# Attention scores from two float32r parts, two heads at a time on half of TensorE's rows, in a fused attention and expert-attention kernel

## The reference

```
x = x + attn(layernorm(x)):
    q, k, v = x @ Wq.T, x @ Wk.T, x @ Wv.T          16 heads of 16 features
    softmax(q k^T / 16) v, per head, then @ Wo.T + bo
x = x + ffn(layernorm(x)):                           8 heads of 64 features, 5 experts
    wv = top2mask(x Ws) * sigmoid(x Ws);  v = sum_e wv_e (x Wv_e)
    softmax(q k^T / 8) v, per head
    out = sum_e top2mask(x Wd)_e (attn Wo_e)
```

## Time and profile before

| | us |
|---|---|
| runs | 6238.3, 6242.69 (median 6240.49) |
| profiled execution | 6241.76 |
| its span | 6239.9 |
| granted TensorE clock, mean | 0.877 of full speed |
| busy PE / PEld / DVE / ACT / POOL | 5111.2 / 2215.6 / 3996.4 / 2947.7 / 3752.6 |

### The profile page before, as it was taken

How to read it: one execution, slowest core, us unless ns; L and a number is a source line. 1 busy time by engine, 2 the same in 40 slices (tenths; PEclk the granted TensorE clock), 3 DMA queues, 4 the chain that set the end, 5 groups by cost and what they waited for, 6 DMA issues and landing times.

```text
span 6239.9 us, 62744 instructions
## 1 busy us (share of the span) xinstructions
PE 5111.2 (82%) x20352; PEld 2215.6 (36%) x20352; DVE 3996.4 (64%) x6573; ACT 2947.7 (47%) x5313; POOL 3752.6 (60%) x3078
## 2 busy tenths in 40 slices
PE   5778888888888888888888888888888888888876
PEld 1233333333333333333333333333333333333333
DVE  4466666666666666666666666666666666666542
ACT  1344444544544544544544544544545444545542
POOL 0046656666656666656666656666656666656688
PEclk7689888989888989889989889989889989889887
DMA  2111111111111111111111111111111111111000
GB/s 67 44 33 42 34 28 41 38 28 39 36 28 38 41 28 37 39 28 37 42 28 37 39 28 37 42 28 35 40 28 37 41 29 34 42 28 34 18 8 7
DMA packets 151479, 213.70 MB, mean 34 GB/s; under 512 B 23408, under 2 KB 125104, under 8 KB 150960
## 3 DMA queue, kind: packets, MB, share of 16 engines
q1 hardware_dynamic: 151152, 209.69, 12.6%
HBM read 139.87 MB, written 69.73 MB: 34 GB/s over the span
## 4 chain that ended last, share of the span: by engine, by line
PE 43%; DVE 22%; POOL 12%; issue 11%; ACT 11%; DMA 0%; SPq 0%; POOLq 0%; ACTq 0%; DVEq 0%
PE bank L190 8%; PE bank L214 6%; POOL s_acc L726 5%; DVE s_mxa L681 4%; PE bank L224 4%; PE bank L276 4%; PE bank L202 4%; DVE s_mxf L693 3%; PE bank L343 3%; ACT s_pa L496 3%; POOL s_vh L744 3%; DVE s_xn L597 3%; DVE s_xn L542 3%; PE bank L332 2%; DVE s_k L642 2%
## 5 line engine op out<-in xcount | busy, mean ns | idle before, releaser
L496 ACT ACTIVATE s_pa<-bank 128x512 f32<-128x512 f32 x2048 | 1227.2, 599 | 2054.2 <-PE bank L214 2051.1
L681 DVE TENSOR_REDUCE s_mxa<-bank 128x1 f32<-128x512 f32 x2048 | 1389.1, 684 | 935.3 <-PE bank L224 930.1
L726 POOL TENSOR_TENSOR s_acc<-s_pf 128x512 f32<-128x512 f32 x256 | 326.9, 1278 | 1375.5 <-PE bank L363 1250.7
L214 PE MATMUL bank<-s_qs,s_ks 99*128 99x512 bf16 x2048 | 858.5, 419 | 329.0 <-ACT s_pa L496 323.0
L726 POOL TENSOR_TENSOR s_acc<-s_acc,s_pf 128x512 f32<-128x512 f32 x512 | 650.7, 1277 | 680.3 <-ACT s_pf L509 678.6
L224 PE MATMUL bank<-s_ks,s_qs 96*128 96x512 bf16 x2048 | 862.6, 421 | 227.7 <-DVE s_mxa L681 195.3
L190 PE MATMUL bank<-s_pa,s_v 128*17 128x512 f32 x4096 | 686.3, 748 | 305.4 <-DVE s_t L569 235.9
L509 ACT ACTIVATE s_pf<-bank 128x512 f32<-128x512 f32 x1024 | 611.6, 597 | 415.6 <-PE bank L237 227.7
L693 DVE TENSOR_REDUCE s_mxf<-bank 128x1 f32<-128x512 f32 x1024 | 698.4, 683 | 140.3 <-PE bank L254 138.6
L214 PEld LDWEIGHTS bank<-s_qs,s_ks 99*128 99x128 bf16 x2048 | 200.5, 98 | 1633.8 <-issue 983.2
L768 POOL TENSOR_TENSOR s_uu<-s_uu,s_pu 128x640 f32<-128x640 f32 x448 | 695.5, 1552 | 35.1
(11 more groups left out here) (98 smaller groups left out, 7110.5 us busy)
## 6 DMA issues: line engine op xcount, KB each, us to landing
w_parts<-s_pt SPq DMA_DIRECT2D x128, 384.0 KB, 2.8
s_ks<-w_parts SPq DMA_DIRECT2D x768, 64.0 KB, 2.9
s_qs<-w_parts SPq DMA_DIRECT2D x128, 192.0 KB, 3.6
s_xn<-in_x SPq DMA_DIRECT2D x32, 512.0 KB, 5.0
s_qs<-w_parts SPq DMA_DIRECT2D x128, 128.0 KB, 3.7
s_xa<-in_x SPq DMA_DIRECT2D x32, 512.0 KB, 4.3
out_y<-s_xa SPq DMA_DIRECT2D x32, 512.0 KB, 3.0
s_qs<-w_parts SPq DMA_DIRECT2D x128, 64.0 KB, 3.6
```

Source lines behind the costliest of these rows:

```text
L214: e.matmul(bk[:, :], ks[0:99, c, h, 128 * kc:128 * kc + 128], qs[0:99, c, h, :], start=True, stop=True).then_inc(p_aexp, 1)
L496: e.activation(pa[:, k % 6, :], Xa.at["x", b, n, g][:, :], ACT.Exp, scale=0.0625).then_inc(a_aexp, 1)
L681: e.tensor_reduce(mxa[:, c, g, h:h + 1], Ma.at["m", b, n, g][:, :], AX.X, ALU.max, negate=True).then_inc(v_amax, 1)
L726: e.tensor_tensor(acc[:, u, :], was, pf[:, k % 6, :], ALU.add).then_inc(g_add, 1)
```

## The change

Attention's q and k are split into two float32r parts (not three bfloat16). A head then has 48 rows, 50 with the two parts of its maximum, and two heads lie on rows 0 to 49 and 64 to 113 of `qs` and `ks`. The two heads' scores go to the two banks of one double-bank buffer: `mb` for maxima, `xb` for exponentials. One DVE reduction or one ACT exponential covers both banks (1024 columns). The second block uses the same two buffers. A slot has three parts. All other results take turns in two banks. The orders and offsets change with it: scores come first in each part on ACT and DVE; the fourfold DVE transposes of the attention output are at slots 4, 8, 12, 16 (g = 1); POOL's reciprocal roots are in the slot of the statistics; ACT's copies of q and k of the second block are four at g = 0 and four at g = 1; v is computed at -5 into a doubled `v32`; the second q, k projections have one slot more between them; the column sums' additions are one slot later; the last projection is one slot later.

```diff
-        xt = sb("xt", [128, 2, 2, 512])
+        xt = sb("xt", [128, 2, 512])
-        pt = sb("pt", [128, 3, 512], BF)
-        qs = sb("qs", [128, 2, 8, 512], BF)
-        ks = sb("ks", [128, 2, 8, 512], BF)
+        pt = sb("pt", [128, 2, 512], F32R)
+        qs = sb("qs", [128, 8, 512], F32R)
+        ks = sb("ks", [128, 8, 512], F32R)
-        pa = sb("pa", [128, 6, 512])
+        pa = sb("pa", [128, 3, 2, 512])
-        bank = [ctx.enter_context(nc.psum_tensor(f"bank{i}", [128, 512], F32)) for i in range(8)]
-        oa, of = bank[6], bank[7]
+        mb, xb = [ctx.enter_context(nc.psum_tensor(n, [128, 2, 512], F32)) for n in ("maxb", "expb")]
+        bank = [ctx.enter_context(nc.psum_tensor(f"bank{i}", [128, 512], F32)) for i in range(2)]
+        oa, of = [ctx.enter_context(nc.psum_tensor(n, [128, 512], F32)) for n in ("oab", "ofb")]
-        parts = dram("parts", [2, 2, 2, 3, 128, 512], BF)
+        parts = dram("parts", [2, 2, 2, 2, 128, 512], F32)
-        CUTS = [[(0, 0, 48), (48, 0, 32), (80, 0, 16)],
-                [(0, 0, 16), (16, 0, 16), (32, 0, 16), (48, 16, 16), (64, 16, 16), (80, 32, 16)]]
+        CUTS = [[(0, 0, 32), (32, 0, 16)], [(0, 0, 16), (16, 0, 32)]]
-        FM = [(0, 2), (2, 5), (5, 8)]
-        Ma, Mf = Turns(bank[0:2]), Turns(bank[3:5])
-        Xa, Xf = Turns(bank[2:3]), Turns(bank[5:6])
+        FM = [(F - 4, 2), (F - 3, 0), (F - 3, 2), (F - 2, 2)]
+        R = Turns(bank)
+        M, X = Turns([mb]), Turns([xb])
...
         def tensor(e):
...
-                for g in range(4):
+                for g in range(3):
+                    if g < 2 and (r := part_of(s, 0, 16)):
+                        _, before = X.next(None, a_aexp, 32 * b + 2 * n + g + 1)
+                        if before:
+                            w.wait_ge(*before)
+                        for a in range(2):
+                            m = e.matmul(xb[:, a, :], ks[64 * a:64 * a + 50, pr, 128 * kc:128 * kc + 128],
+                                         qs[64 * a:64 * a + 50, pr, :], start=True, stop=True)
+                        m.then_inc(p_aexp, 1)
+                    if g == 2 and (r := part_of(s, F, 16)):
+                        _, before = X.next(None, a_fexp, 16 * b + n + 1)
...
+                    if g == 0 and (r := part_of(s, 1, 16)):
...
+                    if g == 1 and (r := part_of(s, F + 1, 16)):
...
+                    if g < 2 and (r := part_of(s, -10, 16)):
+                        _, before = M.next(None, v_amax, 32 * b + 2 * n + g + 1)
...
+                        for a in range(2):
+                            m = e.matmul(mb[:, a, :], qs[64 * a:64 * a + 48, pr, 128 * i:128 * i + 128],
+                                         ks[64 * a:64 * a + 48, pr, :], start=True, stop=True)
+                        m.then_inc(p_amax, 1)
+                    for i, (off, at) in enumerate(FM):
+                        if at == g and (r := part_of(s, off, 4, 4)):
+                            _, before = M.next(None, v_fmax, 4 * n + i + 1)
...
         def scalar(e):
+                    if g < 2 and (r := part_of(s, 0, 16)):
+                        if k >= 3:
+                            w.wait_ge(p_apv, (k - 3) // 2 + 1)
+                        e.activation(pa[:, k % 3, :, :], xb[:, :, :], ACT.Exp, scale=0.0625).then_inc(a_aexp, 1)
+                    if g == 2 and (r := part_of(s, F, 16)):
+                        e.activation(pf[:, k % 3, :, :], xb[:, :, :], ACT.Exp, scale=0.125).then_inc(a_fexp, 1)
+                    if g < 2 and (r := part_of(s, F - 4, 4, 4)):
+                        z = g
+                        for u in range(2):
+                            e.copy(up, src).then_inc(a_fqk, 1)
+                            e.copy(dn, src).then_inc(a_fqk, 1)
...
         def vector(e):
+                    if g < 2 and (r := part_of(s, -10, 16)):
+                        e.tensor_reduce(mxa[:, c, k % 4, 2 * (k // 4):2 * (k // 4) + 2], mb[:, :, :], AX.X, ALU.max,
+                                        negate=True).then_inc(v_amax, 1)
+                    for i, (off, at) in enumerate(FM):
+                            e.tensor_reduce(mxf[:, pair % 2, i, :], mb[:, :, :], AX.X,
+                                            ALU.max, negate=True).then_inc(v_fmax, 1)
...
-                                e.tensor_tensor(bk[:, :], bk[:, :], pt[:, 0, :], ALU.subtract).then_inc(v_part, 1)
-                                w.wait_ge(a_part, 2 * n + 2)
-                                e.tensor_tensor(pt[:, 2, :], bk[:, :], pt[:, 1, :], ALU.subtract).then_inc(v_part, 1)
+                                e.tensor_tensor(pt[:, 1, :], R.at["qk", b, c, z][:, :], pt[:, 0, :].bitcast(F32),
+                                                ALU.subtract).then_inc(v_part, 1)
...
-                    if g == 0 and (r := part_of(s, 5, 4, 4)):
+                    if g == 1 and (r := part_of(s, 4, 4, 4)):
+                        e.transpose(t1[:, 0, :], oa[:, :]).then_inc(v_tr, 1)
...
         def gpsimd(e):
-                    if g == 0 and (b := batch(s, 20)) is not None:
+                    if g == 1 and (b := batch(s, 19)) is not None:
                         w.wait_ge(v_ln2, 13 * b + 9)
                         e.tensor_tensor(rsf[:, :], vef[:, :], nhalf[:, :], ALU.pow).then_inc(g_rs2, 1)
...
         def sync(e):
+                                    for a in range(2):
+                                        sd = parts[b % 2, z, c].rearrange("s (d p a) n -> a (s d) p n", a=2, p=4)[a]
+                                        for to, fr, k in CUTS[z]:
+                                            e.dma_start((qs, ks)[z][64 * a + to:64 * a + to + k, lo:lo + 2, :].bitcast(F32),
+                                                        sd[fr:fr + k, 2 * u:2 * u + 2, :]).then_inc(d_st[z][c][u], 16)
...
+                            for a in range(2):
+                                e.dma_start(qs[64 * a + 48:64 * a + 50, 4 * c:4 * c + 4, :].bitcast(F32),
+                                            maxa[b % 2, c].rearrange("s (p a) n -> a s p n", a=2)[a]
+                                            ).then_inc(d_mxr[c], 16)
```

More of the change, by code:

```diff
@@ L223, in tensor @@
[L223 to L232 removed]
+                        w.wait_ge(d_fr[pair], 16 * (b + 1))
@@ L257, in tensor @@
-                    if g == 0 and (b := batch(s, -20)) is not None:
-                        for f in range(2):
-                            bk, before = Ma.next(("t1", b, f), a_xt, 2 * b + f + 1)
-                            if before:
-                                w.wait_ge(*before)
-                            w.wait_ge(v_ln1, 13 * b + 13)
-                            for i in range(4):
-                                m = e.transpose(bk[:, 128 * i:128 * i + 128], xn[:, i, 128 * f:128 * f + 128],
-                                                ident[:, :])
-                            m.then_inc(p_t1, 1)
@@ new lines, in tensor @@
+                            m.then_inc(p_fmax, 1)
+                    if g < 2 and (b := batch(s, -20)) is not None:
+                        bk, before = R.next(("t1", b, g), a_xt, 2 * b + g + 1)
+                        if before:
+                            w.wait_ge(*before)
+                        w.wait_ge(v_ln1, 13 * b + 13)
+                        for i in range(4):
+                            m = e.transpose(bk[:, 128 * i:128 * i + 128], xn[:, i, 128 * g:128 * g + 128],
+                                            ident[:, :])
+                        m.then_inc(p_t1, 1)
@@ L272, in tensor @@
+                    for c, offs in enumerate(((-18, -16), (-8, -6))):
+                        for z in range(2):
+                            if g == 1 and (b := batch(s, offs[z])) is not None:
+                                bk, before = R.next(("qk", b, c, z), v_part, 4 * b + 2 * c + z + 1)
                                 if before:
@@ new lines, in tensor @@
+                    if g in (0, 2) and (b := batch(s, -5)) is not None:
+                        i2 = g // 2
+                        bk, before = R.next(("v", b, i2), a_v, 2 * b + i2 + 1)
+                        if before:
+                            w.wait_ge(*before)
+                        w.wait_ge(a_xt, 2 * b + 2)
+                        for i in range(2):
+                            for f in range(2):
+                                tc = 2 * i2 + i
+                                m = e.matmul(bk[:, 256 * i:256 * i + 256], xt[:, f, 128 * tc:128 * tc + 128],
+                                             wv[:, f, :], start=(f == 0), stop=(f == 1))
+                        m.then_inc(p_v, 1)
@@ L365, in tensor @@
-                    if g == 3 and (r := part_of(s, F + 5, 4, 4)):
-                        b, pair = r
-                        bk, before = Ma.next(("ot", b, pair), a_ots, 4 * b + pair + 1)
-                        if before:
-                            w.wait_ge(*before)
-                        w.wait_ge(a_osb, 4 * b + pair + 1)
```

(15 more changed lines are left out.)

653 lines of the change are left out of this document (276 added, 377 removed).

## The result

The changed kernel takes 5804.07 us (median of two runs, 5800.5 and 5807.63) against 6240.49: ratio 0.9301, 95% interval 0.9261 to 0.9341. Its profiled execution took 5807.63 us, span 5805.8, at a mean granted clock of 0.902. The forecast was 5920 in a range of 5600 to 6440: the case (faster, by the order) was right, the gain 5% forecast and 7% measured.

What follows compares the result with a forecast made beforehand. Bound by TensorE's work, stalls behind ACT and DVE blocks, and the clock: 147.7 work + 20 idle + 9.4 clock loss = 177.1 us a period against 187.7; 30 x 10.6 = 318 off 6241.76 us gives 5920, range 5600 to 6440.

Steps and rivals of the forecast that it cites:

- Filling and draining: Start and end of the run, outside the 29 steady periods: counted as about one more period's gain of 10.6 us.
- the pair: Two heads' scores matmuls on TensorE, row tiles side by side: 0.52 us against 0.45 before, +4.5 us a period.
- The way back and the product with v: TensorE's return to 128-row work, 0.19 us each, +5.9 a period; the product's old tiling cost goes, -4.2.
- Stalls of the product with v: TensorE's waits for DVE's transpose of the accumulator: 7.6 us of gaps a period go with the earlier transposes.
- Copies split in halves: ACT's second-block q and k copies, exponential ahead of each half: waits left are 0.4 us in slot 0, 2.3 in slot 12.
- slot 12: 2.3 us idle left at the maxima, plus 1.4 because k waits for q's differences in the two turning banks.
- POOL's roots: Reciprocal roots that DVE's normalizations wait for: ready a part ahead in slot 4, with no separate gain given.
- slot 4: Normalization 2's 5.38 us DVE block delays the maxima from 7.0 to 13.3: 6.2 us idle, nothing gained.
- Masks, slots 8 to 11: DVE's 42 us of work around the top-2 masks against TensorE's 37: 5.5 us idle with waits, 10.2 before.
- rival 2: Slower, because the maxima have one buffer and TensorE waits for reductions: 34.5 us idle a period, 6560 us; chance 0.22.
- Rival 1: The two heads' matmuls don't run side by side: a pair takes 0.63 us, 6130 us in all; chance 0.19.
- Rival 3: Much faster: second weight load hidden, 140.7 us of work, mask and slot 12 stalls absorbed, 15 idle: 5490 us; chance 0.14.

Runs made afterwards that it cites:

- b_order: Kernel before, old scores, with DVE's transpose block and POOL's roots three parts earlier and ACT's q and k copies split over two parts: 5821.59 us, ratio 0.9328.
- b_turn: Kernel before, with only DVE's block that turns and divides the attention output moved three parts earlier: 6023.55 us, ratio 0.9654.
- a_turn_late: Changed kernel, with DVE's transpose block put back to the first part of slots 5, 9, 13, 17: 6097.16 us, ratio 0.9771 to the kernel before.
- b_turn_root: Kernel before, with DVE's transpose block and POOL's two roots three parts earlier, ACT's copies left together: 5813.65 us, ratio 0.9326.
- x_ring: Changed kernel, with the second block's q and k products issued last in their parts and layernorm 1's transposes one part later: 5784.26 us, ratio 0.9272.
- a_single: Changed kernel, with each double-bank reduction and exponential split into two single-bank ones: 5847.68 us, ratio 0.9371 to the kernel before.
- a_same_rows: Changed kernel, with both scores matmuls of a pair reading the same row tile: 6489.77 us, ratio 1.0401 to the kernel before.
- x_spread_fm: x_ring, plus second block's maxima last in their part, the first of them one part later, and normalizations spread over three parts: 5681.90 us, ratio 0.9111.

## Why the prediction was right, and where its sizes were off

- **What bounds it: right.** TensorE's work, stalls behind blocks on DVE and ACT, and the clock. The forecast took 141.5 + 6.2 of work, 20 idle and 9.4 clock; measured 138.4, 23.0 and 12.7. That the period was forecast to 3 us is in part luck: 9.3 us less work than forecast stand against 6.3 more of idle time and clock.
- **Filling and draining: mis-sized.** The forecast is 116 us too high. Of this 61 lie in the 28 periods, at 12.8 us of gain each where 10.6 was forecast. The other 55 lie in filling and draining, which the prediction counted at two periods' worth, 21 us, without looking at them, and which gave 76.6.
- **Within the period, the mis-sized term is the pair.** It was costed at 0.52 us, with the second weight load exposed; it measures 0.43: the loads of two row tiles run side by side. That is 64 x 0.09 = 5.8 us of work a period too much, and 174 us of the forecast's time. The rule that the prediction weighed and set aside (the Trainium skill, TensorE: Matmul & The Clock Gate, section Measured speedup vs the span model) was right on this point: by it the pair was to cost 0.41, and in the trace the two matmuls of the pair at 2618.93 start within 0.01 us of each other, where the prediction's sign was 0.11. The error was to carry the 0.11 us between weight loads to two tiles: those loads share one tile.
- **The way back and the product with v: right in size.** Forecast 0.19 us for each return, measured 0.10 + 0.11. The 0.13 that the product was to lose does not go from its own row: it still takes 0.99 (2619.36 to 2620.35). What goes is the drain ahead of it, visible before as four transposes that take 0.58 us ahead of it (L372) where others of that kind take 0.43:

```profile
3036.48 0.66 PE L372 MATMUL bank<-s_ident,s_osb 128*128 128x128 f32 x4
```

  (the product behind it starts at 3037.06). In sum: before 0.15 + 0.99 and two pairs of 0.45, 2.04 us; after 0.10 + 0.43 + 0.99 + 0.43 + 0.11, 2.06. The scores are a draw, and 141.5 of work should have become 141.5 + 32 x 0.02 = 142.1. It is 138.4: **3.7 us stay unattributed**. b_order, with most gaps gone and the old scores, has 140.9, so 0.6 goes with the gaps and the rest only with the new kernel. The first part fits busy time, which holds the 0.16 us by which a matmul's record outlasts its turn, once ahead of each gap; for the rest there is no row.
- **Stalls of the product with v: right.** 7.6 us went; b_turn and a_turn_late show it from both sides.
- **Copies split in halves: right that little is left (2.0 of the 2.3 in slot 12), wrong as a cause.** b_order against b_turn_root: nothing, with the old scores; with the new ones no run tries it.
- **POOL's roots: named, under-weighed.** The prediction has the root ready a part ahead in slot 4 and slot 11's 4.23 us gap gone, and it was gone. On top of the transposes it is worth 3.3 points, as much as they are; the prediction gave it no number of its own.
- **Slot 4: nearly right, by another path.** Forecast 6.2 us in one wait; 3.19 + 2.36 = 5.5 in two, since y's result stands between q and k in the turning banks. x_ring put them together again as 6.22.
- **Slot 12:** 1.4 forecast for k's turn, 2.60 measured.
- **Masks, slots 8 to 11:** 5.5 forecast, five gaps of 1.37, 0.76, 1.99, 1.07 and 1.01 us measured, 6.2.
- **Not foreseen:** the second block's maxima wait 1.3 us for attention's reduction (2572.47 above), three times a period outside the mask stretch, 4.0 us. This is rival 2 in small. With slot 12's extra 1.2 it makes up more than the 3.0 of idle time missing; turning banks elsewhere cost less than the 2 allowed.
- **Clock:** forecast 0.47 us of loss per us idle, as before; measured 12.7 / 23.0 = 0.55.
- **ACT and DVE: right.** 1.22 and 1.03 us forecast, 1.223 and 1.025 measured; worth 0.75% (a_single), where none was forecast. **Queues: right**: landing in 3.1 us, and DMA is 0% of the chain.

**Rivals.** Rival 1 is refuted: the pair is 0.43, not 0.63, and a_same_rows shows what its world looks like, 6489.77 us, worse than the 6130 worked out, because of the clock. Rival 2's mechanism exists, at 7 us of idle time with the mask stretch's two waits of 1.99 and 1.01, but the total of 23.0 stayed under the 27 from which it would have decided. Rival 3's pair was right, and its sign, loads recorded together, is there; its absorbed stalls and its clock of over 0.95 weren't (0.90); x_spread_fm removes 3.5 us of the stalls.

## What to carry to other kernels

When a change brings new arithmetic and a new order together, price them apart, and look first at which small instruction on a side engine a long block waits for: here moving two tiny reciprocal roots and the block around one transpose gave 6.7 of the 7%, and in the steady periods rewriting the scores gave nothing measurable. Look at filling too, and not only at a period: there the new kernel gained 70 us. A long block on an engine that is 62% busy can be a stall of its own length for whoever is queued behind it (a block of 5.25 us, a gap of 6.22); spreading it over the parts of a slot cut the gap, where x_ring's exchange of its neighbours had only moved the wait. And a load that is serial within one tile says nothing about two tiles: where the trace has no row for the new form, keep the better end of the range in play.

## What the runs showed of the hardware that was not expected

- Weight loads of two 64-row tiles take 0.18 to 0.19 us together; on one tile two take 0.29 (a_same_rows; 64-row loads).
- Going from 128-row work into a row-tiled pair costs about 0.10 us of drain, and coming back about 0.11 us of exposed float32 weight load, by the distances above.
- A busy TensorE does not by itself bring the clock back: in a_same_rows it is granted 1.2 GHz for 30.7 us with 28.0 busy. The loss per us of idle time is 0.47 before and 0.55 after, so it is no constant of the kernel. What decides it stays open.
- DVE's normalization of 128x256 takes 1.02 us an instruction in the changed kernel (4.08 for four, above), 1.34 before and 1.31 in x_ring (5.25 for four), with the same operands. What slows it was not tried. GpSimd is busy beside the fast ones (3.85 of 4.08 us) and the slow ones (5.22 of 5.38) alike, so that alone doesn't part them.
